# A fused attention and ternary FFN layer: the second FFN product begins two slots earlier, VectorE scales one quad of each group

## The reference

```python
x = x + attn(layernorm(x), W_query, W_key, W_value)        # causal, no output projection
x = x + ffn(layernorm(x), w1, conv_w, conv_b, w2)

def weight_quant(w):                       # ternary weights
    scale = 1.0 / clip(mean(abs(w)), 1e-05)
    return clip(round(w * scale), -1, 1) / scale
def act_quant(x):                          # 8 bits, one scale per token
    scale = 127.0 / clip(max(abs(x), axis=-1), 1e-05)
    return clip(round(x * scale), -128, 127) / scale
def ffn(x):
    h = act_quant(x) @ weight_quant(w1).T
    h = silu(depthwise_conv1d(h, conv_w, conv_b))          # 3 taps along the tokens
    return act_quant(h) @ weight_quant(w2).T
```

## Time and profile before

| | us |
|---|---|
| median of 3 runs | 977.31 (977.04 to 978.27) |
| the profiled execution, slowest core | 977.3 |
| its span, core 5 | 975.7 |
| spans of the eight cores | 969.7 to 975.7 |
| PE busy in the span | 889.0 (91%) |
| DVE, ACT, POOL busy | 711.9 (73%), 697.3 (71%), 620.6 (64%) |
| mean DMA rate | 171 GB/s |

### The profile page before, as it was taken

One profiled execution on the slowest core, in us unless ns is written; L12 is line 12 of the kernel. 1 busy time (PEld: TensorE's weight loads), 2 busy tenths in 40 slices (PEclk: granted clock), 3 DMA queues, 4 the chain that ended last, 5 costly groups with the idle time before them and its releaser, 6 DMA issues.

```text
span 975.7 us, 24133 instructions; the slowest of 8 cores (969.7 to 975.7 us)
## 1 busy us (share of the span) xinstructions
PE 889.0 (91%) x7516; PEld 538.3 (55%) x7516; DVE 711.9 (73%) x1173; ACT 697.3 (71%) x1108; POOL 620.6 (64%) x819
## 2 busy tenths in 40 slices
PE   1999899999999989998776699999999999999998
PEld 0454454555554545554654466666666666666443
DVE  2677665566666676669588988989899887877651
ACT  3554698889887888988988678678777777766300
POOL 2220648574655565545546978979799797978650
PEclk9999999999998999999989899999999999999999
DMA  8952666765876777774894323325343223332121
GB/s 262 331 169 91 233 222 214 237 215 181 255 247 218 223 243 250 231 238 191 243 313 162 108 67 118 139 92 173 109 133 128 89 94 124 108 130 88 44 87 44
DMA packets 38891, 166.93 MB, mean 171 GB/s; under 512 B 4977, under 2 KB 5106, under 8 KB 30066
## 3 DMA queue, kind: packets, MB, share of 16 engines
q1 hardware_dynamic: 34354, 148.62, 47.0%
q0 software_dynamic: 4416, 16.78, 5.1%
HBM read 140.22 MB, written 25.17 MB: 170 GB/s over the span
## 4 chain that ended last, share of the span: by engine, by line
PE 75%; DVE 7%; ACT 6%; issue 6%; DMA 3%; POOL 2%; SPq 0%; DVEq 0%; ACTq 0%; POOLq 0%
PE psO L968 21%; PE psM L950 19%; PE psQK L748 11%; PE psS L806 7%; PE psPV L834 6%; PE psV L723 5%; ACT PT L1110 4%; DMA wvst<-wv 2%; DMA w1b<-t1scr 2%; PE psS L816 1%; DVE psD L1543 1%; DVE hs L1524 1%; POOL hs L667 1%; PE psK L748 1%; ACT hs L1159 1%
## 5 line engine op out<-in xcount | busy, mean ns | idle before, releaser
L1110 ACT ACTIVATE PT<-psS,nbias 128x1024 bf16<-128x1024 f32 (+1 forms) x320 | 299.9, 986 | 45.2 <-PE psS L806 27.2
L950 PE MATMUL psM<-xqT,w1b 128*128 128x258 bf16 x2048 | 242.9, 277 | 20.3 <-DVE hs L1524 16.2
L667 POOL TENSOR_TENSOR hs<-hs,tb 128x256 f32<-128x256 f32 x256 | 194.6, 784 | 68.2 <-DVE hs L1524 61.8
L950 PEld LDWEIGHTS psM<-xqT,w1b 128*128 128x128 fp8e4 x2048 | 200.7, 99 | 61.4 <-issue 24.3
L1159 ACT ACTIVATE hs<-psM,convb_s,convw_s 128x256 f32<-128x256 f32 x256 | 147.5, 576 | 86.2 <-PE psM L950 61.4
L676 POOL TENSOR_TENSOR hs<-hs,srow 128x256 f32<-128x256 f32 x240 | 178.5, 777 | 15.5 <-ACT srow L1177 15.4
L1524 DVE SCALAR_TENSOR_TENSOR hs<-psM,convw_s,hs 128x256 f32<-128x256 f32 x256 | 114.8, 476 | 23.7 <-ACT tb L1163 22.6
L1543 DVE TENSOR_REDUCE psD<-hs 128x256 f32<-128x1024 f32 x56 | 109.3, 1952 | 22.0 <-ACT hs L1170 22.0
L748 PE MATMUL psQK<-ln1T,wqkb 128*128 128x512 bf16 x480 | 124.0, 382 | 1.4 <-ACT qkO L1086 0.2
L1163 ACT ACTIVATE tb<-psM,convw_s 128x256 f32<-128x256 f32 x256 | 123.6, 483 | 0.0
L834 PEld LDWEIGHTS psPV<-vaug,PT 128*128 128x128 bf16 x2176 | 92.1, 98 | 50.8 <-issue 25.5
(11 more groups left out here) (147 smaller groups left out, 1052.8 us busy)
## 6 DMA issues: line engine op xcount, KB each, us to landing
wbuf<-w1q SPq DMA_DIRECT2D x32, 1024.0 KB, 6.3
wbuf<-w2p SPq DMA_DIRECT2D x32, 1024.0 KB, 6.7
...
```

Source lines behind the costliest of these rows:

```text
L667: e.tensor_tensor(hs_quad(q)[:, part], hs_quad(q)[:, part], tb_quad(q)[:, part], ALU.add).then_inc(g_add, 1)
L950: inst = e.matmul(psM[j][:, 0:GRP + 2], w1b[:, at:at + 128], xqT[:, x0:x0 + GRP + 2], start=(kc == 0), stop=(kc == 7))
L1110: e.activation(out=pt_unit(u).rearrange("p (h w) -> p h w", w=512)[:, :, 128 * j:512], in_=psS[u % 2][:].rearrange("p (h w) -> p h w", w=512)[
```

## The change

Five things.

1. `second` starts at slot 14, not 16 (`LAG`), and its halves come in another order: for each m first half 0 of both n, then half 1 of both. All 64 halves are still there, so 50 of them now have a slot of the first product beside them, or two more than before, and 14 are left behind it.
2. `OWN = 1`: quad 0 of each group is scaled by VectorE, out of PSUM into an int16 tile `hi`, and then copied to fp16 (`scale_round_h`). GpSimd scales the seven others. Tables `SCALED`, `ROUNDED` and `ADDED` are new: quad 1 is rounded a slot later than before (b = 4), quad 7 at the beginning of the next group, and one `add_out` of a group moves from b = 4 to b = 5. In the last group VectorE scales quads 0, 1, 3, 5, 7 and GpSimd 2, 4, 6. Writers of psNb wait until VectorE has read it.
3. The weight steps of s = 9, 15, 19, 24, 29 move to 11, 16, 20, 25, 30, so the one of s = 9 comes behind `place_bias` at s = 10.
4. The two chains that make the weight scale move from slots 8 to 17 of pairs 2 and 4 to slots 32 to 38.
5. Loads: two `x1t` at slot 2 and one each at slots 6 and 7; `x1g` at slots 12 and 13; `w2T` at slots 4, 6, 8 and 10. Stores of the output and loads of `x1g` have other places in the slots.

```diff
-            STEPS += [UN * hp + s for s in (4, 9, 15, 19, 24, 29, 34, 39)]
+            STEPS += [UN * hp + s for s in (4, 11, 16, 20, 25, 30, 34, 39)]
...
-        SCALED = {2: (0, 1), 3: (2,), 4: (3, 4), 5: (5,), 6: (6,), 7: (7,)}
-        ROUNDED = {3: (0, 1), 4: (2,), 5: (3, 4), 6: (5,), 7: (6,)}
+        SCALED = {2: (1,), 3: (2, 3), 4: (4,), 5: (5,), 6: (6,)}
+        ROUNDED = {3: (0,), 4: (1, 2), 5: (3,), 6: (4, 5), 7: (6,)}
+        OWN = 1
+        LAG = 14
+        ADDED = ((1, 2, 5, 6), (1, 2, 4, 5))
...
-                        for st in range(5, 9):
-                            load_x1t(st)
-                    if G == 0 and b == 3:
+                        load_x1t(5)
+                        load_x1t(6)
+                    if G == 0 and b in (6, 7):
+                        load_x1t(b + 1)
+                    if G == 1 and b in (4, 5):
+                        load_x1g(b - 4)
+                    if 8 * G + b in (4, 6, 8, 10):
                         x1_spilled(e)
-                        load_x1g(0)
-                        load_x1g(1)
-                    if 5 <= 8 * G + b <= 8:
...
+                    if b == 7 and 1 <= G < NGRP:
+                        scale_h(8 * (G - 1) + 7)
...
-            def second(g, b):
-                m, n, half = b // 4, (b // 2) % 2, b % 2
+            def second(k):
+                g, i = divmod(k, 8)
+                m, half, n = i // 4, i // 2 % 2, i % 2
...
+                    e.wait_ge(v_hq, 8 * (g - 1) + OWN)
...
-                    if G >= 2:
-                        second(G - 2, b)
+                    if 0 <= k < 8 * NGRP:
+                        second(k)
...
+            def scale_round_h(q):
+                g = q // 8
+                e.wait_ge(a_srow, g + 1)
+                if q >= 1:
+                    e.wait_ge(v_hq, q)
+                done(e.tensor_tensor(
+                    hi[:].rearrange("p (j s) -> p j s", s=GRP),
+                    hs_quad(q).rearrange("p (j s) -> p j s", s=GRP),
+                    psNb[:, 256:512].unsqueeze(1).to_broadcast(
+                        [128, 4, GRP]), ALU.mult))
+                settled()
+                e.tensor_copy(place_h(q), hi[:]).then_inc(v_hq, 1)
```

More of the change, by code:

```diff
@@ L1568, in token_scale, with place_h @@
                                 ALU.mult).then_inc(v_deq, 1)
[L1570 to L1585 removed]
+            def place_h(q):
+                g = q // 8
                 if q == 0:
@@ L1608, in _ @@
                 for b in range(8):
+                    if b == 0 and 2 <= G <= NGRP:
+                        round_h(8 * (G - 2) + 7)
                     if G < NGRP:
```

100 lines of the change are left out of this document (48 added, 52 removed).

## The result

The changed kernel is slower: 984.64 us median of 4 runs (982.99 to 986.01) against 977.79 us, 1.0068 times the time before, 95% interval 1.0053 to 1.0084. The profiled execution took 986.01 us; its slowest core is core 3.

The account below looks back on a forecast made before the run. TensorE was taken as the bound from 579 to 906 us, with other engines holding it up from 467 to 579. Core 1: 976.7 - 6.5 - 2.3 - 2.5 + 8.1 = 973.5, plus 0.5 for lower clock: 974.0 us, range 965 to 981.

Parts of the forecast that it names:

- S: FFN groups, group 7 and tail: time the new tables add, +8.1 us.
- term 4: FFN groups: a chain through ScalarE's taps brings quad 3 1.4 us late in groups 2 to 6; +8.1 us in all.
- The rival on the other side: VectorE and GpSimd hinder each other at cast and roundings: slower, 980 us, deciding from S = 13.9 on; chance 0.15.
- Term 1: Second product two slots sooner: two halves leave the tail for TensorE's holes in slots 14 and 15; -6.5 us.
- the prediction's own test of 4: Sign that the first three terms are wrong: slot 18 begins, on core 1, less than 4 us earlier.
- Term 2: Attention pairs 4 and 5: ternary step behind the bias ends TensorE's stall; -2.3 us, bounds 0 and -2.8.
- Term 3: FFN slot 5: loads apart win back part of TensorE's 3.71 us wait for weights; -2.5 us.
- The front unchanged: Slots 5 to 13 stay VectorE's, another wait follows the bias wait, Term 2 and Term 3 are 0: 978 us; chance 0.15.
- The prediction's chain: Group 2: from ScalarE's taps at 600.95 through quad 1 and further taps to quad 3 at 616.15 us.
- in each other's way: VectorE and GpSimd clash at the cast and roundings of quads 1 and 3: S = 14.4, 980 us; chance 0.15.
- No stall: FFN groups: ScalarE's taps have slack or VectorE catches up, S is 2 or less: 967 us; chance 0.25.

Follow-up runs that it names:

- front_only: Changed kernel with second product at slot 16 in old order, GpSimd scaling all quads, old tables, quad 7 in its old place: 0.9952 of the kernel before.
- second_old_q1: second_old with quad 1 rounded at b = 3 again: 0.9909 of the kernel before.
- steps_old: Changed kernel with the weight steps back at s = 9, 15, 19, 24, 29: 1.0089 of the kernel before.
- chain_early: Changed kernel with the weight-scale chain back at slots 8 to 17 of head pairs 2 and 4: 1.0054 of the kernel before.
- loads_old: Changed kernel with the loads of slots 2 to 8 as before: 1.0075 of the kernel before.
- second_old: Changed kernel with second product at slot 16, halves in old order, add_out, stores and x1g loads in old places: 1.0012 of the kernel before.
- q1_early: Changed kernel with quad 1 of each group rounded a slot sooner, at b = 3: 0.9968 of the kernel before.

## Why the prediction was wrong

**Sum.** Forecast 974.0, range 965 to 981; measured 984.64. The side was wrong, and the value lies beyond the range. On the mean core the span was to fall by 3.2 us and rose by 7.3. Of these 10.5 us, 6.6 lie from slot 18 on, 2.3 in attention and 1.8 in the front, and 0.2 go the other way ahead of the first mark.

**The step that failed** is S, the sum of term 4: the mechanism was right, the size was not. Forecast were 7.6 us of waits in the groups and 0.5 for group 7 and the tail, 8.1; measured were 10.1 in the groups, 3.0 in group 7 and 1.6 in the tail, 14.7. The larger part of the miss is the 0.5 for group 7 and the tail, where 4.6 came. The rival on the other side named S = 13.9 as the point from which slower decides.

**Term 1 (-6.5) was right in the halves, and at the front of core 1 by luck.** On core 1, where the sum was made, slot 18 begins 2.1 us sooner after slot 0 (115.1 to 113.0), and +0.4 - 2.5 had been forecast; from the span's start it begins 4.4 us sooner (581.93 to 577.55), which passes the prediction's own test of 4. But on the mean core it is 0.3 and 0.5 us, and the front is made of other parts than the forecast's: 1.6 us less by parts 3 to 5 (front_only), 1.4 less by VectorE's scaling and quad 7's new place with quad 1 on time, 1.8 more by quad 1's late slot, 0.9 more by the early start. The late slot was charged in the groups and not here. The tail gained 5.3 of the 6.9 us. What is missing there is the step "it waits some 3 us for quad 7's rounding; but the wait of 1.62 us ... is covered by that. I count 0.5 us": the wait of 3.01 us came and replaces 2.2 us of waits, and on core 5 the clock fell to its lower level for part of the 10 us around it (0.83 granted), which the 0.5 us did not hold.

**Term 2 (-2.3) was right for the bias and wrong in what was charged at nothing.** Slots 8 to 31 of pair 4 fell by 1.4 us, as forecast, and of pair 5 by 0.3. In pair 5 five cores take 26.6 to 26.9 us at clock 1.00 and three 28.0 to 28.2 at 0.94; in second_old_q1, where all are at 1.00, the pair fell by the forecast 0.9. steps_old shows the term in reverse: attention 1.8 us longer than the mean of the runs with the moved steps. But the sentence "Moving the weight-scale chain and the stores costs nothing" failed. At slots 32 to 38 the chain's column sums stand on VectorE behind a ternary step whose load was late. VectorE and TensorE of the changed kernel, core 7, head pair 4:

```profile
317.77 1.28 DVE L1338 TENSOR_SCALAR t1s<-wbuf,smalls 128x2048 int16<-128x2048 f32 x1 [3.41 <-DMA wbuf<-w1q]
...
320.38 0.16 DVE L1350 TENSOR_REDUCE smalls<-smalls 128x1 f32<-128x16 f32 x1
...
320.79 0.19 PE L791 MATMUL psN<-smalls,onesf_s 128*1 128x1 f32 x2 [1.57 <-DVE smalls L1350]
```

On this core TensorE waited 1.57 us for sums that the prediction called slots ahead of their users. On the mean core the way from slot 31 of pair 4 to slot 8 of pair 5 grew by 1.0 us, that from slot 8 of pair 2 to slot 8 of pair 3 by 0.4, and that from slot 31 of pair 3 to slot 8 of pair 4 by 0.2 (by 0.3 in chain_early, so not by the chain). This took back the 1.7 us of pairs 4 and 5 in this execution: attention came to 0.0. Over the runs the chain costs about 1 us.

**Term 3 (-2.5) was right in kind.** Against loads_old the spread loads save 1.9 us of front on the mean core and up to 3.3, and every core now takes 113.0 us. *The front unchanged* is out as a rival, since steps_old and loads_old take 1.8 and 1.9 us away again; that terms 2 and 3 came to little on the mean core has the other causes named above.

**Term 4 (+8.1) had the right mechanism at little more than half the price.** ScalarE's second wait, the late quad 3 and one stall per group are all there. What the mechanism lacks is that quad 1's late slot also costs the groups 5.0 us when TensorE does not ask for quad 3 early (second_old against second_old_q1). VectorE, ScalarE and GpSimd of the changed kernel, core 5, group 4:

```profile
711.87 1.21 DVE L1598 TENSOR_TENSOR hi<-hs,psNb 128x1024 int16<-128x1024 f32 x1
713.25 0.47 DVE L1604 CAST hqb<-hi 128x1024 f16<-128x1024 int16 x1 [0.17 <-DVE hi L1598]
...
718.43 1.97 DVE L1555 TENSOR_REDUCE psD<-hs 128x256 f32<-128x1024 f32 x1 [0.33 <-ACT hs L1182]
720.50 0.42 DVE L1558 TENSOR_TENSOR amf<-psD,amf 128x256 f32<-128x256 f32 x1
720.84 1.81 DVE L1611 TENSOR_SCALAR hqb<-hs 128x1024 f16<-128x1024 f32 x2
...
726.24 1.97 DVE L1555 TENSOR_REDUCE psD<-hs 128x256 f32<-128x1024 f32 x1
728.32 0.42 DVE L1558 TENSOR_TENSOR amf<-psD,amf 128x256 f32<-128x256 f32 x1
728.66 1.20 DVE L1611 TENSOR_SCALAR hqb<-hs 128x1024 f16<-128x1024 f32 x1
...
713.92 0.56 ACT L1171 ACTIVATE hs<-psM,convb_s,convw_s 128x256 f32<-128x256 f32 x1 [3.89 <-PE psM L958]
...
717.16 1.10 ACT L1182 ACTIVATE hs<-hs 128x1024 f32<-128x1024 f32 x1
...
721.73 0.56 ACT L1171 ACTIVATE hs<-psM,convb_s,convw_s 128x256 f32<-128x256 f32 x1 [2.35 <-DVE hqb L1611]
...
728.57 3.24 POOL L684 TENSOR_TENSOR hs<-hs,srow 128x256 f32<-128x256 f32 x4
```

The wait at 713.92 is put down to psM, but psM's matmuls had begun at 710.22, and the taps start 0.2 us behind the cast's end; in second_old the same wait reads `DVE hqb L1604`.

From the start of the taps of b = 4 (713.92) to quad 3 on TensorE (730.11) it takes 16.2 us. The prediction's chain has 15.2 for the same way (600.95 to 616.15). The missing 1.0 us: silu to maximum 0.17 us, twice (717.16 + 1.10 to 718.43); quad 1 at 0.89 for 0.85; quad 3's rounding at 1.20 for 0.85, where GpSimd's multiplication begins 0.1 us before it; 0.25 us to TensorE. The price of 0.85 left out what the rows held: the 1.87 us for two roundings are 0.74 and 1.21. The start of the chain came 0.4 us sooner than forecast (3.7 us behind the start of psM's matmuls for 4.1). That is not the cast's merit: VectorE began the multiplication 1.65 us behind them and not 2.17 (599.00 - 596.83), and from there to the taps it takes 2.05 us for the forecast 1.95. A stall that is the small difference of two ways of 16 us had an error of its own size: 1.8 us per group for 1.4.

Group 7, which has the same chain, was not worked out but counted with the tail at 0.5 us. It has a wait of 1.9 to 2.4 us and, on some cores, lower clock behind it, 3.0 us on the mean; and its cast takes 1.0 us on all eight cores, where those of groups 2 to 6 take 0.45 to 0.54.

**The rival "in each other's way"** came nearest in time, and a part of its mechanism shows. Quad 3's rounding took 1.20 us, begun 0.09 us behind one of GpSimd's multiplications. Quad 1's took 0.68, begun 0.09 us ahead of one (720.84 and 720.93), and there the multiplication took 1.18 us instead of 0.73. The cast, to which the rival gave the price, was not held up in groups 2 to 6 (0.45 to 0.54 us on all cores), but it was in slots 12 and 60 (0.95 to 1.03). The Trainium skill, "SBUF — State Buffer", section "Who interferes with whom", lets either engine be blocked, the one that comes second; the trace agrees in these two roundings. VectorE's multiplication out of PSUM, which by the prediction's reading of that section is safe, took 1.21 or 1.22 us in all its 96 executions. **"No stall"** is nearly what second_old_q1 has: the second product back at slot 16 in its old order and quad 1 on time, with 0.3 to 0.7 us of wait in three groups of core 5.

**What the change was worth part by part**, from the runs: parts 3 to 5 alone 0.9952; part 2 with quad 1 a slot sooner another 0.4% (second_old_q1); quad 1's late slot +5.0 us in the groups, 1.8 in the front and 2.6 in the tail, where a wait of 1.7 us for the maxima is back (second_old against second_old_q1); the early start on top of it +5.1 in the groups, 3.0 in group 7 and 0.9 in the front, for 5.3 in the tail (the changed kernel against second_old). With quad 1 on time the early start still costs 7.3 us of front and groups for 2.0 us of tail (q1_early against second_old_q1).

Attention of one and the same code varies from 378.9 us (core 5) to 383.7 (core 7). Of these 4.8 us, 0.4 lie in slots 8 to 31 of pair 4, 2.9 on the way from there to slot 8 of pair 5, where core 7 has waits of 1.57, 0.98 and 0.82 us, and 1.6 in slots 8 to 31 of pair 5, where core 7's granted clock is 0.94 and core 5's 1.00. Not settled is why the waits and the lower clock fall on some cores and not on others; no experiment was made on it.
